# Adaptive-norm transformer layer on one Trainium2 core: another order of the first FFN's blocks and of the weight splits around its end

## What is computed

```
x = x + attn(cond(x))        # attn = approx_out + FFN 1
x = x + ffn(cond2(x))        # FFN 2
cond(x)  = x @ W.T + 2 * (low-rank experts, top 2 of 8, gated)
attn(h)  = series terms + silu(h @ gate.T) * (h @ up.T) @ down.T   # 1248 hidden features
cond2(x) = x @ W.T + b + 2 * (low-rank update, adapter by sequence)
ffn(h)   = silu(h1) * h3, then w2, each linear with a low-rank update   # 1376 hidden
```

## Time and profile before

| What | us |
|---|---|
| Median of three runs | 456.35 |
| Lowest and highest | 456.27, 457.39 |
| The profiled execution | 457.57 |
| Its span (first to last instruction) | 455.9 |
| TensorE (PE) matmuls busy in it | 446.5 |
| VectorE (DVE) busy | 324.5 |
| ScalarE (ACT) busy | 211.6 |
| POOL busy | 29.2 |

### The profile page before, as it was taken

The page is one execution under the profiler, slowest core; times in us unless marked ns, Lnnn a source line. Parts: engine busy times, 40 slices in busy tenths (PEclk is TensorE's granted clock), DMA queues, the critical chain, the costliest instruction groups (busy, mean ns, idle before and its releaser), DMA issues.

```text
span 455.9 us, 5562 instructions
## 1 busy us (share of the span) xinstructions
PE 446.5 (98%) x2009; PEld 364.0 (80%) x2009; DVE 324.5 (71%) x471; ACT 211.6 (46%) x324; POOL 29.2 (6%) x51
## 2 busy tenths in 40 slices
PE   8999999999999999999997999999999999999997
PEld 7788888888777888768884888888888888888886
DVE  5755799657987678886568555989963468887731
ACT  6364442355664456553644555556542124565300
POOL 1004100000010100004300000000000000000000
PEclk9999999999999999999999899999999999999999
DMA  8407700136574564637243101222110232112022
GB/s 288 136 0 224 187 1 0 34 94 156 123 197 121 138 155 127 169 89 192 70 128 107 39 0 47 63 58 76 42 47 24 69 92 65 46 47 69 1 93 92
DMA packets 20299, 42.28 MB, mean 93 GB/s; under 512 B 2672, under 2 KB 2944, under 8 KB 20272
## 3 DMA queue, kind: packets, MB, share of 16 engines
q1 hardware_dynamic: 16992, 34.35, 23.4%
q0 software_dynamic: 3280, 7.58, 9.5%
HBM read 39.82 MB, written 2.10 MB: 92 GB/s over the span
## 4 chain that ended last, share of the span: by engine, by line
PE 87%; DVE 8%; ACT 2%; DMA 1%; issue 1%; ACTq 0%; DVEq 0%
PE PS L1676 14%; PE PS L1541 14%; PE PS L1542 14%; PE PS L1543 14%; PE PS L1677 13%; PE PS L1678 13%; DVE G L922 2%; DVE WU L922 1%; DMA raw<-in_pieces 1%; ACT G L481 1%; PE PS L1862 1%; PE PS L1604 1%; DVE X L1377 1%; ACT WU L481 1%; DVE T L1107 1%
## 5 line engine op out<-in xcount | busy, mean ns | idle before, releaser
L1676 PE MATMUL PS<-HT,WU 128*128 128x512 f32 x266 | 103.8, 390 | 0.7 <-DVE WU L922 0.7
L1677 PE MATMUL PS<-HT,WU 128*128 128x512 f32 x266 | 103.6, 390 | 0.0
L1678 PE MATMUL PS<-HT,WU 128*128 128x512 f32 x266 | 103.5, 389 | 0.0
L481 ACT ACTIVATE WU<-raw 128x256 fp32r<-128x256 f32 (+2 forms) x55 | 49.0, 897 | 34.0 <-PE PS L1678 18.1
L922 DVE TENSOR_TENSOR WU<-raw,WU 128x256 fp32r<-128x256 f32 (+2 forms) x56 | 56.5, 1013 | 5.1 <-ACT WU L481 5.0
L1676 PEld LDWEIGHTS PS<-HT,WU 128*128 128x128 f32 x266 | 50.0, 188 | 11.7 <-DVE WU L922 1.5
L481 ACT ACTIVATE PS<-PS 128x512 f32<-128x512 f32 x46 | 26.8, 582 | 68.6 <-PE PS L1678 65.2
L1678 PEld LDWEIGHTS PS<-HT,WU 128*128 128x128 f32 x266 | 49.9, 188 | 10.5
L1677 PEld LDWEIGHTS PS<-HT,WU 128*128 128x128 f32 x266 | 50.0, 188 | 10.1
L922 DVE TENSOR_TENSOR G<-T,G 128x1024 fp32r<-128x1024 f32 (+2 forms) x46 | 43.9, 968 | 18.0 <-ACT G L481 17.1
L481 ACT ACTIVATE G<-T 128x1024 fp32r<-128x1024 f32 (+2 forms) x47 | 39.8, 856 | 20.0 <-DVE T L1038 6.8
(11 more groups left out here) (170 smaller groups left out, 705.9 us busy)
## 6 DMA issues: line engine op xcount, KB each, us to landing
raw<-in_pieces SPq DMA_DIRECT2D x87, 256.0 KB, 3.7
raw<-in_parts SPq DMA_DIRECT2D x14, 512.0 KB, 3.6
raw<-in_parts POOLq DMA_DIRECT2D x14, 384.0 KB, 4.9
X<-in_x SPq DMA_DIRECT2D x8, 256.0 KB, 5.1
out_x<-X SPq DMA_DIRECT2D x7, 256.0 KB, 2.0
su_raw<-in_stk_up POOLq DMA_DIRECT2D x6, 192.0 KB, 2.7
T<-in_lora_b POOLq DMA_DIRECT2D x16, 32.0 KB, 2.1
ga_raw<-in_lora_a POOLq DMA_DIRECT2D x8, 32.0 KB, 3.4
```

The costliest lines, as they stand in the source:

```text
L481: return nc.scalar.activation(o, i, ACT.Copy)
L1676: pe.matmul(bank, w[:, 1, cols], hi, start=start and kc == 0, stop=False, skip_group_check=not start)
L1677: pe.matmul(bank, w[:, 0, cols], low, start=False, stop=False, skip_group_check=not start)
L1678: mm = pe.matmul(bank, w[:, 0, cols], hi, start=False, stop=kc == 1, skip_group_check=not start)
```

## The change

- `BLOCKS`: u4 stands before d0, d1, and u8 before d2, d3. The list is u0 to u4, d0, d1, u5 to u8, d2, d3, u9.
- `enter_down` is gone: all blocks have the ordinary order on TensorE, ScalarE and VectorE. In it the split of T4 stands behind the big weight split. T1 of an even chunk before a down block is split in the second down block, as are the tail operands of chunk 8. `x_out` a stands behind the big weight split.
- The last block is written out: `last` on ScalarE and VectorE. S13 and S2's first piece are split at the end of block 12, S2's others, the tail weights and W2's pieces in block 13. `x1(h)` alternates additions and splits.
- The buffer has six slots for these pieces (the two new ones lie where the sums of even blocks were), the pieces come in the order S13, S2, tail, W2, and two operands in G have other places.
- SP: a block's first piece is loaded with the 256 columns used only (128 KB for 256 KB), and ahead of the load of the sums, no longer behind it.

No matmul is added or removed.

```diff
-BLOCKS = [("u", 0), ("u", 1), ("u", 2), ("u", 3), ("d", 0), ("d", 1), ("u", 4), ("u", 5), ("u", 6), ("u", 7),
-          ("d", 2), ("d", 3), ("u", 8), ("u", 9)]
+BLOCKS = [("u", 0), ("u", 1), ("u", 2), ("u", 3), ("u", 4), ("d", 0), ("d", 1), ("u", 5), ("u", 6), ("u", 7),
+          ("u", 8), ("d", 2), ("d", 3), ("u", 9)]
...
+P_ONE, P_TWO, BLOCK_PIECES = {}, {}, []
 for _q in range(len(BLOCKS)):
-    P_BLOCK.append(len(SLOT))
-    SLOT += [0, 1] if _q % 2 == 0 else [3, 2]
-P_TAIL = len(SLOT)
-P_S13 = P_TAIL + 2
+    for _n in range(2):
+        (P_ONE, P_TWO)[_n][_q] = len(SLOT)
+        BLOCK_PIECES.append((_n, _q))
+        SLOT.append(((0, 1), (3, 2))[_q % 2][_n])
+P_S13 = len(SLOT)
 P_S2 = P_S13 + 1
-P_W2 = P_S2 + 4
-SLOT += [0, 1, 2, 3, 0, 1, 2, 3, 0, 1, 2]
+P_TAIL = P_S2 + 4
+P_W2 = P_TAIL + 2
+SLOT += [0, 1, 4, 5, 3, 2, 0, 1, 4, 5, 3]
...
-            return G[:, 4 * (c - TAIL) + 2 * h + 1]
+            return G[:, ((1, 7), (3, 5))[c - TAIL][h]]
...
+                k, q = BLOCK_PIECES[p - P_FFN] if P_FFN <= p < P_S13 else (None, None)
+                if k == 1:
                     if q > 1:
-                        sp.wait_ge(w_ready, P_BLOCK[q - 2] + 2)
+                        sp.wait_ge(w_ready, P_TWO[q - 2] + 1)
                     sp.dma_start(sum_region(q), parts[q][:, 0:1024]).then_inc(sum_in[q % 2], 16)
                 sp.wait_ge(w_ready, before_in_slot(p) + 1)
-                sp.dma_start(raw_slot(p), pieces[p]).then_inc(raw_in[SLOT[p]], 16)
+                if k == 0:
+                    a11 = slice(256 * (q % 2), 256 * (q % 2) + 256)
+                    sp.dma_start(raw_slot(p)[:, a11], pieces[p][:, a11]).then_inc(raw_in[SLOT[p]], 16)
+                else:
+                    sp.dma_start(raw_slot(p), pieces[p]).then_inc(raw_in[SLOT[p]], 16)
...
             def steady1(q):
+                c = number(q - 1) if is_up(q - 1) else None
+                odd = c is not None and c % 2 == 1
                 part1_hi1(q + 1, p4_done, q)
                 copy_bc1(q, *c_free(q - 1))
-                g_first(q)
+                if odd:
+                    two_hi(c, ("T2", "T3"), (T2, 1), T[:, 6:8, :])
+                elif c is not None and is_up(q):
+                    two_hi(c, ("T1",), (B11, T1), T[:, 2:7:4, :])
                 copy_e1(q)
-                g_later(q, 2)
+                if odd:
+                    b2_hi(c)
                 part2_hi1(q + 1)
+                if second_down(q):
+                    c = number(q - 2)
+                    if c == TAIL:
+                        for h in range(HALVES):
+                            tail_g_hi(c, h)
+                    else:
+                        two_hi(c, ("T1",), (B11, T1), T[:, 2:7:4, :])
                 silu1(q, 0)
-                g_later(q, 3)
-                next_a(q)
+                if odd:
+                    t4_hi(c)
+                if q == LAST - 1:
+                    s13_hi()
+                    s2_hi(0)
+                copy_ab1(q + 1, *b_free(q - 1))
                 silu1(q, 1)
...
+            def last(q):
+                s2_hi(1)
+                copy_bc1(q, *c_free(q - 1))
+                s2_hi(2)
                 copy_e1(q)
-                g_later(q, 2)
-                copy_ab1(q + 1, *b_free(q - 1))
-                copy_bc1(q, *c_free(q - 1))
-                part2_hi1(q + 1)
-                g_later(q, 3)
+                s2_hi(3)
+                tail_hi(0)
+                tail_hi(1)
+                silu1(q, 0)
+                for k in range(2):
+                    w_hi(P_W2 + k, W2[k])
+                silu1(q, 1)
+                for h in range(HALVES):
+                    tail_g_hi(C1 - 1, h)
+                for k in range(2, KC):
...
+                    if odd:
+                        t2_t3_sums(c)
+                    elif c < TAIL:
+                        t1_sum(c)
+                sums1(q + 1)
+                part1_lo1(q + 1)
+                if odd:
+                    two_lo(c, "T2", (T2, 1), T[:, 6:8, :])
+                elif c is not None and is_up(q):
+                    two_lo(c, "T1", (B11, T1), T[:, 2:7:4, :])
+                add_b1(q)
+                if odd:
+                    two_lo(c, "B21", (B21, 1), T[:, 2:4, :])
+                    t4_sum(c)
+                add_d1(q)
+                part2_lo1(q + 1)
+                if odd:
+                    t4_lo(c)
+                if second_down(q):
+                    c = number(q - 2)
+                    if c == TAIL:
+                        for h in range(HALVES):
+                            tail_g_lo(c, h)
                     else:
-                        mul0_1(c)
-                        if c < TAIL:
-                            g_sum(c)
-                    sums1(q + 1)
-                    part1_lo1(q + 1)
-                    if up and c >= TAIL:
-                        g_lo1(c, 0)
-                        g_lo1(c, 1)
-                    elif up:
-                        g_lo1(c, c % 2)
-                    add_b1(q)
-                    if pair:
-                        g_lo1(c, 2)
-                        g_sum4(c)
-                if not is_up(q):
-                    x_out(q, "a")
-                add_d1(q)
-                if pair and not first_down(q):
-                    g_lo1(c, 3)
-                part2_lo1(q + 1)
+                        two_lo(c, "T1", (B11, T1), T[:, 2:7:4, :])
                 if is_up(q):
                     mul1_1(number(q))
                 else:
+                    x_out(q, "a")
                     x_out(q, "d")
                     x_out(q, "b")
+                if q == LAST - 1:
+                    s13_lo()
+                    s2_lo(0)
+            def last(q):
+                x_out(q - 1, "c")
+                s2_lo(1)
+                s2_lo(2)
+                add_b1(q)
+                s2_lo(3)
+                tail_lo(0)
+                tail_lo(1)
+                add_d1(q)
+                for k in range(2):
+                    w_lo(P_W2 + k, W2[k])
+                mul1_1(C1 - 1)
+                mul0_1(C1 - 1)
+                for h in range(HALVES):
+                    tail_g_lo(C1 - 1, h)
+                for k in range(2, KC):
+                    w_lo(P_W2 + k, W2[k])
...
+                steady1(q)
+            last(LAST)
...
+                x1_add(h, 0)
+                for c in range(1, KC):
+                    x1_add(h, c)
+                    x1_lo(h, c - 1)
+                x1_lo(h, KC - 1)
...
-            s2_lo(3)
-            for k in range(KC):
-                w_lo(P_W2 + k, W2[k])
...
-                if q < LAST and not first_down(q + 1):
+                if q < LAST:
                     p1_1(q + 1, *a_free(q - 1))
                 p3_1(q)
                 p4_1(q)
```

More of the change, by code:

```diff
@@ L125 @@
 B12 = T4
+G_SUM, G_SPLIT = {}, {}
+for _c in range(0, TAIL, 2):
+    G_SUM[_c, "T1"] = 3 * _c // 2 + 1
+    G_SPLIT[_c, "T1"] = 2 * _c + 1
+    for _n, _names in enumerate((("T2", "T3"), ("T4",))):
+        for _name in _names:
+            G_SUM[_c + 1, _name] = 3 * _c // 2 + 2 + _n
+    for _n, _names in enumerate((("T2", "T3"), ("B21", "B22"), ("T4",))):
+        for _name in _names:
+            G_SPLIT[_c + 1, _name] = 2 * _c + 2 + _n
+for _c in range(TAIL, C1):
+    for _h in range(2):
+        G_SPLIT[_c, _h] = max(G_SPLIT.values()) + 1
+G_SPLITS = max(G_SPLIT.values())
 BANK_A, BANK_B, BANK_C, BANK_E = ((2, 4), (0, 2)), ((3, 5), (1, 3)), (1, 5), (0, 4)
@@ L324, in before_in_slot @@
         def before_in_slot(p):
-            return max(q for q in range(p) if SLOT[q] == SLOT[p])
+            return max([q for q in range(p) if SLOT[q] == SLOT[p]] or [P_TWO[LAST - 1]])
         def term_count(h, m):
@@ L384, in number, with second_down @@
             return BLOCKS[q][1]
-        def first_down(q):
-            return q <= LAST and not is_up(q) and is_up(q - 1)
+        def second_down(q):
+            return not is_up(q) and not is_up(q - 1)
         def a_free(q):
@@ new lines, in steady1 @@
+            def steady1(q):
+                c = number(q - 1) if is_up(q - 1) else None
+                odd = c is not None and c % 2 == 1
+                if c is None:
+                    x_out(q - 1, "c")
+                else:
+                    mul0_1(c)
+                    if odd:
[21 more added lines that the diff above has]
+                            tail_g_lo(c, h)
+                    else:
+                        two_lo(c, "T1", (B11, T1), T[:, 2:7:4, :])
@@ L2054, in first_ffn @@
                                        for j in rows[k]], axis=1) for k in range(2)]
-            got += two
+            blocks.append(two)
             (a11, a21), (a12, a22) = ([t[:, :256], t[:, 256:]][::-1 if q % 2 else 1] for t in two)
             parts.append(np.concatenate([a21, a11, a12, a22, a22, a21, a22], axis=1))
-        return got + list(down[TAIL:]), parts
+        return [blocks[q][n] for n, q in BLOCK_PIECES], list(down[TAIL:]), parts
     def second_ffn():
```

(4 more changed lines are left out.)

234 lines of the change are left out of this document (79 added, 155 removed).

## The result

| What | us |
|---|---|
| Kernel before, median of four runs beside it | 456.31 (455.31 to 457.39) |
| Changed kernel, median of four runs | 448.38 (448.29 to 448.96) |
| Ratio | 0.983, 95% interval 0.981 to 0.985 |
| Profiled execution before, its span | 457.57, 455.9 |
| Profiled execution after, its span | 448.42, 446.7 |

The change makes the kernel 1.7% faster. The forecast was 447.0; the range held the time. The fall between the two profiled executions, 9.15 us, is the 9.3 of the sum; the medians fell by only 7.9. A second error is one of cause: what made the loss at the end of the FFN.

What follows compares the result with a forecast made beforehand. TensorE, busy 98% of the span, bounds the kernel; its stalls in the changed part lose 11.2 us. -2.60 - 2.67 - 5.92 + 1.9 = -9.3 us, from the median 456.35 to 447.0 us; range 445.0 to 450.4.

Steps and rivals of the forecast that it cites:

- First entry: First entry into a down-projection, 121.15 to 146.42: its 2.60 us of TensorE loss goes to 0.
- Second entry: Second entry into a down-projection, 181.10 to 205.98: its 2.67 us of TensorE loss goes to 0.
- SP and POOL: Loads of a block's first piece and sums: sums still land 1.8 us before their reader on VectorE; cost 0.
- End of the FFN: From the FFN into the following linear layer: splits made before the X additions remove 5.92 us of loss; bounds -5.9, -2.9.
- Block 13: Last block: the moved splits delay VectorE and cause three stalls of 0.3, 0.5, 1.1, together +1.9 us; bounds 0, +3.5.
- the margin that T4's place gives: Blocks after an odd chunk: T4's split behind the big weight split lets that split end at 8.91, before 9.32; margin 0.4 us.
- the up block as cover: Entries: an ordinary up block before the down-projection readies all operands of the pair a block earlier; entries lose 0.
- Number 2: Rival: VectorE's arrears never reach TensorE in block 13; -11.2 us, 445.1; chance 0.10.
- Number 3: Rival: the clock falls in or after block 13; 447.0 + 1.6 = 448.6; chance 0.10.
- The rule of the Trainium skill: Frequent short idles may alternate the clock; block 13's three stalls would be paid at half rate, sum -7.7 us.
- Rival 4: W2 and tail loads come late, the first low-rank product waits again, half of the 5.9 stays; 449.9; chance 0.09.
- Rivals 5, 6 and 7: Entries keep their loss, 452.3, chance 0.06; no change, 456.3, 0.03; sums' load late, slower, 461.5 at 3.0 late, 0.04.

Runs made afterwards that it cites:

- t4_first: Changed kernel with T4's split moved back ahead of the big weight split in the four blocks after an odd chunk; 451.38 us, ratio 0.988.
- first_entry_old: Changed kernel with u4 back behind d0 and d1, ordinary order of products, T2 and T3 copy moved forward in d0; 461.48 us, ratio 1.010.
- before_slots: Kernel before with only the six slots for the eleven pieces behind the FFN; 452.43 us, ratio 0.991.
- four_slots: Changed kernel with its order of splits, but the eleven pieces behind the FFN in four slots, so loaded late; 449.95 us.
- slots_right: Kernel before with the new block list and entries, old split places at the end, and six slots, pieces' contents in their places; 446.75 us.
- entries_only: Kernel before with the new block list and ordinary block order, but slots, piece order and splits behind the FFN as before; 451.67 us, ratio 0.988.
- after: The changed kernel itself, first series, against the kernel before; median 448.38 us, profiled execution 448.42 us.
- change_again: The changed kernel unaltered, run again in the second series; median 448.67 us, profiled execution 449.27 us.

## Why the prediction was right, and where it was off

| Step | Forecast, us | Profiled after, us |
|---|---|---|
| First entry | -2.60 | -2.60 (loses 0) |
| Second entry | -2.67 | -2.67 (loses 0) |
| SP and POOL | 0 | 0 |
| End of the FFN | -5.92 | -5.86 (from 228.07 to 242.86 it loses 0.06) |
| Block 13 | +1.9 | +2.14 |
| Sum | -9.3 | -9.0; between the profiled executions -9.15 |

**The entries.** Both parts of the argument were tested by themselves: the margin that T4's place gives (`t4_first`, expected 0.3 to 0.6 a block, measured 0.61), and the up block as cover (`first_entry_old`). Two readings of the rows were short, without effect on the sum, since it counts starts. Each entry had a fourth stall, too small for the list: 0.3 us at 144.02 and at 203.80. And the list of waits has two more groups in the part that changes, for G (0.8 us) and for HT (0.2), so 5.6 us and not 4.6.

**The last block.** The working followed VectorE's rows from block 12. VectorE, then two copies of ScalarE, the first of block 12 and the one for the seventh product of block 13, changed kernel:

```profile
218.33 0.68 DVE L1180 TENSOR_TENSOR X<-X,PS 128x512 f32<-128x512 f32 x1
219.04 0.68 DVE L1244 TENSOR_TENSOR S<-raw,S 32x512 fp32r<-32x512 f32 x1
219.65 0.68 DVE L1249 TENSOR_TENSOR S<-raw,S 32x512 fp32r<-32x512 f32 x1
220.36 0.69 DVE L1180 TENSOR_TENSOR X<-X,PS 128x512 f32<-128x512 f32 x1
221.08 0.68 DVE L1249 TENSOR_TENSOR S<-raw,S 32x512 fp32r<-32x512 f32 x1
222.23 0.68 DVE L1249 TENSOR_TENSOR S<-raw,S 32x512 fp32r<-32x512 f32 x1 [0.47 <-ACT S L503]
222.94 0.70 DVE L1119 TENSOR_TENSOR PS<-PS,T 128x512 f32<-128x512 f32 x1
223.67 0.68 DVE L1249 TENSOR_TENSOR S<-raw,S 32x512 fp32r<-32x512 f32 x1
224.38 1.29 DVE L938 TENSOR_TENSOR WU<-raw,WU 128x512 fp32r<-128x512 f32 x2
225.60 0.69 DVE L1123 TENSOR_TENSOR T<-PS,T 128x512 f32<-128x512 f32 x1
...
208.21 0.42 ACT L503 ACTIVATE WU<-raw 128x256 fp32r<-128x256 f32 x1 [2.08 <-PE PS L1699]
...
221.08 0.58 ACT L503 ACTIVATE PS<-PS 128x512 f32<-128x512 f32 x1 [4.90 <-DVE X L1180]
```

Block 13's time zero is 217.73 (block 12's, ScalarE's first copy at 208.21, plus 9.52). The copy ran at 3.35, forecast 3.45; the addition before the third product at 5.21, forecast 5.2; the one before the last ended at 8.56, forecast 8.3. The three stalls lose 0.21, 0.60 and 1.25 us, forecast 0.3, 0.5 and 1.1. The last ended 0.26 later than forecast, 0.22 of it because the rows at 223.67 and 224.38 start 0.73 and 0.71 after the one before where I had taken 0.61 (last section). That the copy came out within 0.1 is in part luck. I had put block 12's last addition at 5.75, from block 11 of the kernel before, whose first matmuls hold the stall at 203.80; it ran at 5.44 (213.65). Of these 0.3 us the dearer changes to S and back took 0.2. Block 12 ran to its end without a stall, as forecast.

**The step that was mis-sized** is the last: "from the median the forecast is 447.0". It took the whole 9.3 off the median. But 5.92 of it was the loss of one execution, whose clock had fallen to 0.66 after the stall at X, at a price that the prediction itself put at 1.6 us; and it lay 1.2 over the median, which should have said that the median run had not paid this. The runs settle it. Over the three series the kernel before ran 29 times: ten had a mean granted clock of 0.996 and took 457.59 us on average, nineteen had 0.999 or 1.00 and took 456.26. The profiled execution (457.57) was of the first kind. So the two kinds differ by 1.33 us, near the 1.6 read from the rows; only executions of the first kind have a trace, so that the others had the same stalls and just kept the clock isn't shown. The fall comes in a third of the executions (six of eleven, three of nine, one of nine), and the median of three or four runs can miss it. Where the median has not paid it, the changed kernel cannot save it: 456.35 - (9.3 - 1.3) = 448.35, against 448.38 measured. `before_slots`, which removes the end's stalls, brings the fall to none in five runs.

**The end.** The size was right, the cause only in part. Of the 5.92 us, 0.7 were lost at the low-rank products (241.79 to 244.37), 1.0 at W2's first product, 2.5 at X and 1.6 by the lower clock. The prediction said the loss goes because the splits are made before the additions. That would do (`four_slots`), but the change also releases the loads earlier, which is enough by itself (`slots_right`, `before_slots`), and beside it the moved splits only cost. The hint was in the rows: ScalarE stood 2.20 us at a piece of S2, and longer at W2's last piece, with the addition into X that TensorE waited for at 250.04 behind that piece's split:

```profile
248.03 0.63 ACT L481 ACTIVATE G<-raw 128x512 fp32r<-128x512 f32 x1 [4.18 <-DMA raw<-in_pieces]
```


**The rivals.** Number 2 (no stall in block 13) fell, but its time of 445.1, raised by the 1.3 to 446.4, is where `slots_right` with 446.75 lies; that kernel has no moved splits, so the rival isn't borne out by it. Number 3's time (448.6) is near the result for another reason: the clock in block 13 stayed at 1.00, in the profile and in every run. The rule of the Trainium skill weighed there, "TensorE: Matmul & The Clock Gate", section "A second HAM failure mode: psum-queue depth-cycling", would have frequent short idles bring the lower level; three stalls of 0.2 to 1.25 us in 5 us did not, nor the four of `four_slots`. Rival 4 (late W2 and tail loads) did not occur with six slots. In `four_slots` these loads come late and cost 1.3 us, in the last block and the tail and not at the low-rank product where the rival had them. Rivals 5, 6 and 7 fell.

## What to carry to other kernels

Before moving work on a full engine, ask whether the wait in front of it is for work or for a transfer: here two more buffer slots cost nothing, while a moved split cost its 0.6 us at whatever deadline came next. Subtract only the losses that the median run has: compare the profiled execution's clock and time with the other runs' before its stalls are taken off the median. And a wait shown as 0.34 us cost 0.61 from start to start, so count losses there.

## What the hardware showed that I had not expected

- Behind stalls that lost 0.9 and 2.1 to 2.3 us within 6 us in the traces, the granted clock came down in some executions of the same kernel only: in 10 of 29 for the kernel before, in 3 of 6 for `entries_only` (452.34 against 450.85 on average, 1.5 us). Stalls of 4.4 and 3.0 us brought it down in all four runs of `first_entry_old` (mean clock 0.988 to 0.993).
- A wait of TensorE for one operand costs about 0.27 us more than the idle time shown (0.24 to 0.29 over the waits of these traces at full clock). In `t4_first` idle 0.34 goes with a loss of 0.61: 0.16 of it lies under the end of the matmul before (0.39 long at a pitch of 0.227), and 0.11 more is lost because the second matmul starts 0.33 to 0.34 after the first. So four waits listed as 1.4 us cost 2.4, and a wait too small to be listed lost 0.21 (221.72).
- A VectorE operation on S (32 partitions, from the 33rd or the 65th on) between two on all partitions starts 0.71 to 0.73 us after the row before it, and so does the next full one (218.33, 219.04; 219.65, 220.36, 221.08; 222.23, 222.94, 223.67, 224.38); two on S in a row, or two full ones, are 0.60 to 0.61 apart (219.04 to 219.65). The Trainium skill, "VectorE: DVE Perf Modes", section "Two Vector instructions with no wait between them", has an instruction wait for the end of all earlier ones where its operands start in another quarter of the partitions than those of the one before. The trace agrees: such a row starts 0.03 us after the recorded end of the one before, the others 0.07 ahead of it, which makes 0.1 us at each change.
- The same kernel's start varies by 0.9 us with the moment at which the granted clock reaches 1.00: 3.94 us in the profiled execution of `after`, 6.87 in that of `change_again`.
